# Three additions of products moved into transfers, and two sets of statistics moved to ScalarE

## The chip, the cores and the metric

One Trainium2 chip, and of it one core. The time is the device time of one execution of the whole program in microseconds (us); the smaller is the better. "The median" is that of several executions of one build. The profiled execution is one more, recorded by the hardware profiler.

## What is computed

Two preactivation layers over x of shape (8, 64, 64, 256) in float32. Layer 0 is a deformable convolution with 9 taps, 32 groups of 8 channels, and a grid of offsets and masks made by a depthwise convolution and a projection; layer 1 is a convolution with binarised weights and inputs. Both work on the input after group normalisation and add their result to it.

```python
x = x + dcn(gn(x))        # layer 0
x = x + bin_conv(gn(x))   # layer 1

def dcn(x):               # H = W = 64, G = 32, GC = 8, K = 3
    xdw    = depthwise3x3(x) + dw_b
    om     = xdw @ om_w + om_b                # 27 planes a group: 18 offsets, 9 masks
    value  = x @ vp_w + vp_b
    py, px = base + tap + offset
    sampled = bilinear(value, py, px)         # four neighbours, 0 outside the image
    out    = sum_k sampled_k * mask_k         # over the 9 taps
    return out @ op_w

def gn(v, G=32, eps=1e-5):                    # mean and variance over an image's pixels
    return (g - mean(g)) / sqrt(var(g) + eps) # and the 8 channels of a group
```

## The kernel before

Layer 0 takes 3400 of the 3858 us, in `layer0`. Each of the 8 images is cut into 4 steps (n, j), 32 steps in all. A step has 256 pixel columns (TOK) of each of the 4 quarters of the image, and 9 taps k = 0 to 8. The partitions hold 32 groups for each of the 4 quarters. Offsets stay within one pixel of the tap, so that the 9 taps with their neighbours fall on 5 x 5 shifts: the kernel makes one weight plane for each shift (`wsum`) and then 25 products uv = 0 to 24 of `val` and such a plane, which TensorE adds up. If an offset is larger, another routine, `layer0_any_offset`, would do the work instead; here it doesn't run.

Every engine has its own program, written out in the order in which it runs, and they meet at semaphores. In one step:

- **VectorE**, for each tap k: `mask_rows` (L965) multiplies the weights of a tap in y by its mask, `products` (L979) multiplies them by those in x, straight into `wsum` where a shift is new and into `prod` where one is already there. For taps 1, 2, 3, 6, 7 (`SENT_TAPS`) the part in `prod` is added to `wsum` by a transfer; for 4, 5 and 8 by VectorE (L1007). The products of the next tap wait for it. Between these pieces `multiply` (L1026) makes two or three of the 25 products a tap: `SAMPLES_AT` says which. Products 0 to 12 are made in taps 4 to 8 and 13 to 24 in taps 0 to 3 of the step that follows; product 12 is the last instruction of a step. Each product, 128 x 2048 elements, goes into one of 4 buffers of `pv` in turn and waits until TensorE has read what was there.
- VectorE also takes statistics: in tap 0 four rows over `xres` for the group normalisation of layer 1 (`statistics`, L1036), and in steps 0, 1 and 2 of an image four rows for each half of 128 channels of the next image (`sums_ahead`, L925), loaded ahead into `acc` and `acc_t`; a chain of small instructions (`scales_ahead`) turns these into scales.
- **TensorE**, for each tap: two offset products for the tap after next (`offsets`, L751), the first addition of this tap (`add`, L796: 16 transposing matmuls into PSUM), the third offset product, then one unit of the depthwise convolution of the next step (taps 0 to 3, L722) or of its values (taps 4, 5, 7, 8, L735; one unit each, two each in the last step of an image), the transposition back (tap 4, L764) and the projection (taps 5 and 6, L777), and last the other additions of the tap.
- **ScalarE**, for each tap: the hats, that is the weights in x and y, from the offset products two taps ahead (L585 to L599), then the evictions of TensorE's depthwise, value, transposed and projected units, and the normalisation of the input for the depthwise convolution (`tri`, L540: four instructions of 1024 elements in tap 8, four of 512 in taps 1 and 2). In tap 4 it evicts the 25-fold sum into `acc` (`summed`, L606).
- **GpSimd** issues the transfers that add: `wsum` += `prod` (L472), `xres` += x (L462), and the loads of the image ahead (L455). **SyncE** issues the other loads and the stores of the result, x2.

Layer 1 follows, after all images of layer 0; the change does not touch it.

## Time and profile before

| | us |
|---|---|
| median of 3 executions | 3857.94 |
| lowest, highest of them | 3854.49, 3858.15 |
| the profiled execution, its own time | 3859.76 |
| its span in the trace | 3858.0 |
| TensorE, VectorE, ScalarE, GpSimd busy | 3628.5, 3510.0, 2286.0, 565.0 |
| transfers | 470.35 MB |

In the rows below, PE is TensorE's matmuls, PEld its weight loads, DVE is VectorE, ACT is ScalarE, POOL is GpSimd. L1026 is line 1026 of the kernel. A row of a window gives the stretch in us from the start of the span and its length; then for each engine the busy us and, in brackets, the number of instructions; then the granted TensorE clock as a share of full speed, the mean busy share of the 16 DMA engines, and GB/s. A group of instructions gives line, engine, operation, what is written from what, the shapes and the count; after the first bar the busy us and the mean ns of one; after the second the idle time just before them and who ended it. A row of the timeline gives start and duration in us, the engine, the line and the instruction, and in square brackets the idle time before it with its releaser. Durations overlap the next row by a tenth of a microsecond or so, so that distances are taken from start to start. A GB/s row gives the rate in 40 equal slices of its window.

### The profile page before, as it was taken

What the parts mean: (1) busy time and instruction counts of PE and PEld (TensorE: products, weight loads), DVE (VectorE), ACT (ScalarE), POOL (GpSimd) and SP (SyncE); (2) the same over time, 40 slices, a digit from 0 to 9 for tenths busy, and PEclk for the clock granted to TensorE, in tenths of its full rate; (3) what the DMA queues carried; (4) which work ended last, traced back from release to release, by engine and by line L of the source; (5) the groups of instructions that cost most, each with busy time, mean ns of one, the idle gap of its engine ahead of it and who ended that gap; (6) DMA issues with size and microseconds to landing.
All of it is one profiled execution on the core that took longest, in us unless ns stands there. A gap on an engine that the chain in (4) does not pass through costs nothing. (4 is left out here: it accounts for less than half of the span.)

```text
span 3858.0 us, 90635 instructions
## 1 busy us (share of the span) xinstructions
PE 3628.5 (94%) x37696; PEld 2369.5 (61%) x37696; DVE 3510.0 (91%) x2757; ACT 2286.0 (59%) x4547; POOL 565.0 (15%) x412
## 2 busy tenths in 40 slices
PE   4899999999999999999999999999999999858998
PEld 2566666666666666666666666666666666623333
DVE  4899999999999999999999999989999999948776
ACT  5556665666666665666556666665566666235554
POOL 0011111101111111111111001111111111104444
PEclk9999999999999999999999999999999999979999
DMA  6454565445555555455545555555544554345563
GB/s 177 100 111 102 110 125 132 101 111 116 124 120 109 114 123 115 94 108 127 131 99 119 112 121 114 107 122 131 118 100 97 106 107 94 52 158 199 209 215 147
DMA packets 319939, 470.35 MB, mean 122 GB/s; under 512 B 37244, under 2 KB 242684, under 8 KB 313736
## 3 DMA queue, kind: packets, MB, share of 16 engines
q0 software_dynamic: 94080, 196.11, 28.4%
q1 hardware_dynamic: 224584, 266.07, 23.2%
q8 instruction: 298, 4.88, 0.5%
q10 hardware_dynamic: 832, 2.10, 0.1%
q14 instruction: 145, 1.19, 0.1%
HBM read 262.53 MB, written 67.41 MB: 86 GB/s over the span
## 5 line engine op out<-in xcount | busy, mean ns | idle before, releaser
L1026 DVE TENSOR_TENSOR pv<-val,wsum 128x2048 f32<-128x2048 f32 x800 | 1811.2, 2286 | 21.4 <-ACT xdw L557 14.6
L796 PEld LDWEIGHTS ps_add<-ident,pv 128*128 128x128 f32 x12800 | 1401.2, 142 | 356.0 <-issue 223.7
L796 PE MATMUL ps_add<-ident,pv 128*128 128x128 f32 x12800 | 1527.2, 275 | 70.9 <-DVE pv L1026 62.7
L751 PE MATMUL ps_om<-xdw,omw 128*32 128x256 f32 x13824 | 868.4, 384 | 30.4 <-ACT hat L587 29.4
L585 ACT ACTIVATE hat<-ps_om,omb 128x256 f32<-128x256 f32 x576 | 276.0, 479 | 551.2 <-PE ps_om L751 501.9
L979 DVE TENSOR_TENSOR prod<-hat,mwy 128x1536 f32<-128x1536 f32 (+1 forms) x384 | 526.0, 1397 | 82.9 <-DMA wsum<-prod 61.8
L472 POOL DMA_DIRECT2D wsum<-prod x192 | 226.0, 1254 | 2556.8 <-DVE wsum L979 2556.8
L751 PEld LDWEIGHTS ps_om<-xdw,omw 128*32 128x32 f32 x13824 | 391.2, 109 | 330.2 <-issue 95.5
L589 ACT ACTIVATE msk<-ps_om,omb 128x256 f32<-128x256 f32 x288 | 137.0, 476 | 401.4 <-PE ps_om L751 399.3
L965 DVE TENSOR_TENSOR mwy<-hat,msk 128x768 f32<-128x768 f32 x288 | 274.4, 953 | 94.3 <-ACT hat L599 94.3
L722 PE MATMUL ps_bg<-tri,diag 128*32 128x512 f32 x3024 | 346.5, 592 | 11.9 <-ACT tri L551 11.9
L540 ACT ACTIVATE tri<-tri,gn_tri 96x1024 f32<-96x1024 f32 (+1 forms) x376 | 330.0, 951 | 4.7 <-ACT gn_tri L508 4.5
L735 PE MATMUL ps_bg<-win,vpw 128*32 128x256 f32 x4992 | 294.4, 381 | 0.0
L587 ACT ACTIVATE hat<-ps_om,omb 128x256 f32<-128x256 f32 x576 | 281.4, 489 | 0.0
L586 ACT ACTIVATE hat<-ps_om,nomb 128x256 f32<-128x256 f32 x576 | 276.7, 480 | 0.0
L979 DVE TENSOR_TENSOR wsum<-hat,mwy 128x768 f32<-128x768 f32 (+2 forms) x288 | 257.3, 893 | 2.4 <-DVE pv L1026 1.0
L777 PE MATMUL ps_bg<-acc_t,opw 128*128 128x512 f32 x512 | 238.4, 606 | 1.8 <-ACT acc_t L614 0.7
L735 PEld LDWEIGHTS ps_bg<-win,vpw 128*32 128x32 f32 x4992 | 162.8, 111 | 108.9 <-issue 2.5
L1007 DVE TENSOR_TENSOR wsum<-wsum,prod 128x1536 f32<-128x1536 f32 x192 | 226.0, 1219 | 0.0
L1730 POOL TENSOR_TENSOR c_x<-c_x,c_res 128x1024 f32<-128x1024 f32 x64 | 170.4, 2666 | 341.4 <-ACT c_res L1614 341.4
L722 PEld LDWEIGHTS ps_bg<-tri,diag 128*32 128x32 f32 x3024 | 98.6, 111 | 185.6 <-issue 164.6
L1683 PE MATMUL ps_p<-c_over,c_kw 128*128 128x512 bf16 x768 | 189.5, 397 | 19.9 <-ACT c_res L1608 19.9
(134 smaller groups left out, 2622.7 us busy)
## 6 DMA issues: line engine op xcount, KB each, us to landing
wsum<-prod POOLq DMA_DIRECT2D x160, 768.0 KB, 7.1
tri<-in_x_dram SPq DMA_DIRECT2D x725, 128.0 KB, 2.9
win<-in_x_dram SPq DMA_DIRECT2D x144, 256.0 KB, 3.6
x<-xres SPq DMA_DIRECT2D x128, 256.0 KB, 5.1
xres<-in_x_dram POOLq DMA_DIRECT2D x124, 256.0 KB, 8.4
out_dram<-c_x SPq DMA_DIRECT2D x31, 1024.0 KB, 4.5
c_x<-x SPq DMA_DIRECT2D x30, 1024.0 KB, 5.3
c_box<-box_d SPq DMA_DIRECT2D x16, 1024.0 KB, 7.4
```

The costliest lines, as they stand in the source:

```text
L540: last = nc.scalar.activation(v, v, ACT.Identity, bias=gn_tri[0:KROWS, j % 2, 2 * c + 1, h:h + 1], scale=gn_tri[0:KROWS, j % 2, 2 * c, h:h ...
L585: nc.scalar.activation(hat[:, par, a, 1, :], d, ACT.Abs, bias=b).then_inc(abs_done, 1)
L586: nc.scalar.activation(hat[:, par, a, 0, :], d, ACT.Relu, bias=nb, scale=-1.0)
L587: nc.scalar.activation(hat[:, par, a, 2, :], d, ACT.Relu, bias=b).then_inc(om_free, 1)
L722: mm = nc.tensor.matmul(out[:, :, :, o0:o1], diag[:, h, c, kx, :], src, start=kx == 1, stop=kx == 2)
L735: mm = nc.tensor.matmul(ps_bg[G * q:G * q + G, par, ci * TOK:(ci + 1) * TOK], vpw[:, h, 2 * cp + ci, :], win_of(n, j, i // V_UNITS)[:, h, ...
L751: mm = nc.tensor.matmul(ps_om[G * q:G * q + G, (par + i) % 2, 0:TOK], omw[:, h, comp, :], xdw[:, j % 2, h, q, :], start=h == 0, stop=h == ...
L777: mm = nc.tensor.matmul(ps_bg[:, par, :], opw[:, h, P * oh:P * oh + P], acc_t[:, h, 512 * tb:512 * tb + 512], start=h == 0, stop=h == CH - 1)
L796: mm = nc.tensor.matmul(ps_add[:, tb, c, :], pv[:, (j + uv) % PBUF, c, P * tb:P * tb + P], consts["ident"][:, :], start=uv == 0 and c % 4 ...
L965: nc.vector.tensor_tensor(mwy[:, :, :], hat[:, par, 1, :, :], msk[:, par, :].unsqueeze(1).to_broadcast([P, 3, TOK]), ALU.mult)\
L979: return nc.vector.tensor_tensor(dst, hat[:, par, 0, c:d, :].unsqueeze(1).to_broadcast(shape), mwy[:, a:b, :].unsqueeze(2).to_broadcast(sh ...
L1026: nc.vector.tensor_tensor(pv[:, (j + uv) % PBUF, :, :].rearrange("p c (r w) -> p c r w", w=W), val[:, :, SR * j + u:SR * j + u + SR, v:v + ...
```

## The change

Four things change, all in layer 0.

Products 0 and 1, 2 and 3, and 10 and 11 are added in pairs by a transfer within `pv` (`add_pair`), issued by GpSimd, before TensorE sees the sum; TensorE adds 22 times instead of 25. `pv` has five buffers, and product uv goes into buffer uv modulo 5. The product that takes the buffer of the first of a pair (5, 7, 15) waits for the transfer; every other one waits for TensorE's addition of what lies there (16 for the addition of the sum of 10 and 11).

Both sets of statistics are taken by ScalarE, each as one pass for the sum and one for the sum of squares, in place of VectorE's rows: those of the image ahead at the end of taps 7 and 0 (`sums_ahead`), those of `xres` at the end of taps 1 and 2 (`statistics`). The image ahead has only one buffer, `acc_t`, so its second half is loaded after the first has been summed, and both halves after the fourth projection. The sums of products are evicted into `xres` (`acc` is a view of it), so that eviction waits for the stores of x2 from there.

The order of the additions is written out in `ADDS_AT`, apart from that of the products.

```diff
-PBUF = 4
+PBUF = 5
+PAIRED = {1: 0, 3: 2, 11: 10}
+PAIRS = list(PAIRED)
+ADDS_AT = [(13, 14, 11, 15), (16, 17, 18), (19, 20, 21), (22, 23, 24), (), (1,), (4, 3, 5, 6), (7, 8, 9), (12,)]
...
+                def add_pair(n, j, uv):
+
+                    s = STEPS * n + j
+                    pool.wait_ge(pv_full, SHIFTS * s + uv + 1)
+                    at_least(pool, pair_added, 16 * (len(PAIRS) * s + PAIRS.index(uv)))
+                    nc.gpsimd.dma_start(pv[:, (SHIFTS * j + uv) % PBUF, :, :], pv[:, (SHIFTS * j + PAIRED[uv]) % PBUF, :, :],
+                                        accum_op=ALU.add).then_inc(pair_added, 16)
...
                         for k in SENT_TAPS:
+                            if k == 6:
+                                add_pair(n, j, 1)
+                                add_pair(n, j, 3)
+                            add_products(n, j, k)
                             if k == 6 and j < CH and n < NI - 1:
-                                load_ahead(n, j, 0, "back3")
-                            add_products(n, j, k)
+                                load_ahead(n, j, 0, "project3")
+                        if (n, j) != (0, 0):
+                            add_residual(*previous(n, j), unit(n, j, "project3", NI) + 1)
                         if j < CH and n < NI - 1:
                             load_ahead(n, j, 1, "project3")
-                        if (n, j) != (0, 0):
-                            add_residual(*previous(n, j), unit(n, j, "project3", NI) + 1)
+                        add_pair(n, j, 11)
...
                 def summed(s):
-                    act.wait_ge(add_done, SHIFTS * (s + 1))
+                    act.wait_ge(add_done, ADDS * (s + 1))
+                    at_least(act, x2_stored, 16 * Q * s)
...
+                    for oh in halves:
+                        for i, kind in ((0, ACT.Identity), (1, ACT.Square)):
+                            nc.scalar.activation(spare[:, :, :], xres[:, oh, :, :], kind, bias=pivot2[:, oh:oh + 1],
+                                                 accum_out=x2_sums[:, oh, i, j:j + 1]).then_inc(stats2, 1)
+                            act.wait_ge(stats2, 2 * CH * s + 2 * oh + i + 1)
...
+                    nc.scalar.activation(ahead, ahead, ACT.Identity, bias=pivot[:, j:j + 1],
+                                         accum_out=x_sums[:, half, j, 0:1]).then_inc(centred, 1)
+                    act.wait_ge(centred, i + 2 + half)
+                    nc.scalar.activation(ahead, ahead, ACT.Square, accum_out=x_sums[:, half, j, 1:2]).then_inc(sums_made, 1)
...
+                        if k == AHEAD_AT and j < CH and has_next(n):
+                            sums_ahead(n, j, 0)
+                        if k == 0 and j in (1, 2) and has_next(n):
+                            sums_ahead(n, j - 1, 1)
+                        if k in (1, 2) and not is_step(n, j, 0, 0) and not is_step(n, j, 0, 1):
+                            statistics(*previous(*previous(n, j)), (k - 1,))
...
-                    if not isinstance(s, int) or s > 0 or uv >= PBUF:
-                        dve.wait_ge(add_done, SHIFTS * s + uv - PBUF + 1)
+                    used, in_step = (uv - PBUF, s) if uv >= PBUF else (uv - PBUF + SHIFTS, s - 1)
+                    if used in PAIRED.values():
+                        dve.wait_ge(pair_added, 16 * (len(PAIRS) * in_step + list(PAIRED.values()).index(used) + 1))
+                    elif not isinstance(s, int) or in_step >= 0:
+                        dve.wait_ge(add_done, ADDS * in_step + ADDED.index(used) + 1)
```

TensorE's program at the end of a step, before: taps 7 and 8 and the start of tap 0 of the next step. L751 are offset products, L796 additions (16 matmuls each), L735 a unit of values, L722 the depthwise unit.

```order
L796 MATMUL ps_add<-ident,pv 128x128 x32
L751 MATMUL ps_om<-xdw,omw 32x256 x16
L796 MATMUL ps_add<-ident,pv 128x128 x16
L751 MATMUL ps_om<-xdw,omw 32x256 x8
L735 MATMUL ps_bg<-win,vpw 32x256 x16
L796 MATMUL ps_add<-ident,pv 128x128 x32
L751 MATMUL ps_om<-xdw,omw 32x256 x16
L796 MATMUL ps_add<-ident,pv 128x128 x16
L751 MATMUL ps_om<-xdw,omw 32x256 x8
L722 MATMUL ps_bg<-tri,diag 32x512 x4
L722 MATMUL ps_bg<-tri,diag 32x8x63 x8
L796 MATMUL ps_add<-ident,pv 128x128 x32
```

The same place in the changed kernel, where L861 are the additions, L813 the offset products, L797 the values and L784 the depthwise unit:

```order
L861 MATMUL ps_add<-ident,pv 128x128 x32
L813 MATMUL ps_om<-xdw,omw 32x256 x16
L861 MATMUL ps_add<-ident,pv 128x128 x16
L813 MATMUL ps_om<-xdw,omw 32x256 x8
L797 MATMUL ps_bg<-win,vpw 32x256 x16
L813 MATMUL ps_om<-xdw,omw 32x256 x16
L861 MATMUL ps_add<-ident,pv 128x128 x16
L813 MATMUL ps_om<-xdw,omw 32x256 x8
L784 MATMUL ps_bg<-tri,diag 32x512 x4
L784 MATMUL ps_bg<-tri,diag 32x8x63 x8
L861 MATMUL ps_add<-ident,pv 128x128 x48
```

Tap 8 had three additions, 10 ahead of the third offset product and 11 and 12 behind the values; now it has one, 12, ahead of the third offset product, and tap 0 has four, 13 early and 14, 11, 15 at its end.

GpSimd's program for one step with a load ahead, before: taps 1 and 2 in the first row, then tap 3, a load, taps 6 and 7, a load and the residual.

```order
L472 DMA wsum<-prod 128x3x512 x2
L472 DMA wsum<-prod 128x2x768
L455 DMA acc<-in_x_dram 128x2048
L472 DMA wsum<-prod 128x2x768 x2
L472 DMA wsum<-prod 128x512
L455 DMA acc_t<-in_x_dram 128x2048
L462 DMA xres<-in_x_dram 128x2x256 x4
```

The same in the changed kernel, with the semaphores that each row waits for:

```order
L487 DMA wsum<-prod 128x3x512 [waits wsum_added,prod_done] x2
L487 DMA wsum<-prod 128x2x768 [waits wsum_added,prod_done]
L495 DMA pv<-pv 128x2048 [waits pair_added,pv_full] x2
L487 DMA wsum<-prod 128x2x768 [waits wsum_added,prod_done]
L470 DMA acc_t<-in_x_dram 128x2048 [waits bg_full]
L487 DMA wsum<-prod 128x2x768 [waits wsum_added,prod_done]
L487 DMA wsum<-prod 128x512
L477 DMA xres<-in_x_dram 128x2x256 [waits bg_free]
L477 DMA xres<-in_x_dram 128x2x256 x3
L470 DMA acc_t<-in_x_dram 128x2048 [waits sums_made,bg_full]
L495 DMA pv<-pv 128x2048 [waits pair_added,pv_full]
```

Two pairs now stand ahead of tap 6's transfer, the first load ahead has moved behind it, and the third pair stands at the end of the step, behind the residual and the second load.

## Rows read from the trace of the kernel before

**Rows 1.** The page, busy time of the engines (share of the span, instructions)
```profile
PE 3628.5 (94%) x37696; PEld 2369.5 (61%) x37696; DVE 3510.0 (91%) x2757; ACT 2286.0 (59%) x4547; POOL 565.0 (15%) x412
```
**Rows 2.** Windows: 27 steps; product 16 to step's end; a stretch of layer 1
```profile
255.00:3050.98 2795.98, 2719.48 (x30269) 1859.71 (x30262) 2665.73 (x1999) 1739.81 (x3616) 336.99 (x294) 1.00 0.53 114
...
1213.59:1300.28 86.69, 85.70 (x978) 57.83 (x980) 81.12 (x57) 54.17 (x112) 11.97 (x10) 1.00 0.57 121
...
3500.00:3512.00 12.00, 8.33 (x32) 3.23 (x31) 11.90 (x13) 2.38 (x4) 3.31 (x2) 0.86 0.75 260
```
**Rows 3.** VectorE's groups of instructions in those 27 steps, 255 to 3051 us
```profile
L1026 DVE TENSOR_TENSOR pv<-val,wsum 128x2048 f32<-128x2048 f32 x675 | 1528.8, 2285 | 6.5 <-PE ps_add L796 6.4
L979 DVE TENSOR_TENSOR prod<-hat,mwy 128x1536 f32<-128x1536 f32 (+1 forms) x324 | 443.8, 1397 | 74.1 <-DMA wsum<-prod 60.5 <-issue 9.0 <-DVE var L950 1.2
...
L1036 DVE BATCH_NORM_STATS2 bs<-xres 128x6 f32<-128x512 f32 x108 | 66.6, 679 | 0.8
L925 DVE BATCH_NORM_STATS2 bs<-acc_t 128x6 f32<-128x512 f32 x52 | 32.1, 680 | 0.0
...
L1052 DVE TENSOR_REDUCE scratch<-over_sum 128x1 f32<-128x9 f32 x28 | 4.3, 155 | 0.0
```
**Rows 4.** Timeline, VectorE: start of a step, its product 16, start of the next
```profile
1198.73 2.56 DVE L979 TENSOR_TENSOR wsum<-hat,mwy 128x2304 f32<-128x2304 f32 x1
...
1208.68 2.46 DVE L1036 BATCH_NORM_STATS2 bs<-xres 128x6 f32<-128x512 f32 x4
...
1213.59 2.28 DVE L1026 TENSOR_TENSOR pv<-val,wsum 128x2048 f32<-128x2048 f32 x1
...
1300.46 2.56 DVE L979 TENSOR_TENSOR wsum<-hat,mwy 128x2304 f32<-128x2304 f32 x1 [0.18 <-DVE pv L1026]
```
**Rows 5.** Timeline, TensorE: tap 8 of one step, tap 0 of the next
```profile
1404.55 1.91 PE L735 MATMUL ps_bg<-win,vpw 128*32 128x256 f32 x32
1406.39 3.71 PE L796 MATMUL ps_add<-ident,pv 128*128 128x128 f32 x32
...
1411.89 1.97 PE L796 MATMUL ps_add<-ident,pv 128*128 128x128 f32 x16
1413.79 1.07 PE L751 MATMUL ps_om<-xdw,omw 128*32 128x256 f32 x16
1414.68 2.73 PE L722 MATMUL ps_bg<-tri,diag 128*32 128x512 f32 x24
1417.34 3.71 PE L796 MATMUL ps_add<-ident,pv 128*128 128x128 f32 x32
```
**Rows 6.** Timeline: ScalarE's `tri` blocks and hats at that place; TensorE waiting for hats
```profile
1407.76 4.64 ACT L540 ACTIVATE tri<-tri,gn_tri 96x1024 f32<-96x1024 f32 x4 [0.20 <-ACT gn_tri L508]
1412.31 0.45 ACT L585 ACTIVATE hat<-ps_om,omb 128x256 f32<-128x256 f32 x1
...
1206.59 0.45 ACT L585 ACTIVATE hat<-ps_om,omb 128x256 f32<-128x256 f32 x1
...
1207.81 1.07 PE L751 MATMUL ps_om<-xdw,omw 128*32 128x256 f32 x16 [1.42 <-ACT hat L587]
```
**Rows 7.** Timeline, VectorE: products of taps 4, 8, 6 and 7, waits for transfers
```profile
932.50 2.36 DVE L979 TENSOR_TENSOR prod<-hat,mwy 128x1536 f32<-128x1536 f32 x2 [0.79 <-DMA wsum<-prod]
...
770.73 2.36 DVE L979 TENSOR_TENSOR prod<-hat,mwy 128x1536 f32<-128x1536 f32 x2 [1.46 <-DMA wsum<-prod]
...
1263.94 1.75 DVE L979 TENSOR_TENSOR prod<-hat,mwy 128x1536 f32<-128x1536 f32 x1
...
1274.46 2.36 DVE L979 TENSOR_TENSOR prod<-hat,mwy 128x1536 f32<-128x1536 f32 x2 [0.42 <-DMA wsum<-prod]
```
**Rows 8.** A transfer's median time to landing; tap 7's transfers, issue, and window 1277.4:1286
```profile
wsum<-prod POOLq DMA_DIRECT2D x160, 768.0 KB, 7.1
...
1277.45 2.12 POOL L472 DMA_DIRECT2D wsum<-prod  x2 [9.40 <-DVE wsum L979]
...
GB/s 0 0 0 0 0 0 0 38 171 186 143 214 186 186 214 157 214 186 214 171 186 171 200 214 214 200 181 143 181 219 210 162 181 133 19 10 10 76 0 0
```

159 lines of the change are left out of this document (88 added, 71 removed).

## The prediction, made before the changed kernel was run

> **What bounds the kernel now.** I read the page's busy shares first: TensorE 94%, VectorE 91%, ScalarE 59% [rows 1]. Two nearly full engines mean that neither may be shortened alone, so next come the windows. The 27 steps between the first and last VectorE row that ends a step (the group of 28 in [rows 3]) take 2796.0 us, so 103.55 us a step; in them TensorE is busy 2719.5 (100.7 a step) and VectorE 2665.7 (98.7 a step) [rows 2]. What VectorE waits for there is small and mostly the transfers that add into `wsum`: 60.5 us in all, 2.2 a step [rows 3]. So both engines are close to the bound in turn, and a cheaper step needs both to get shorter and the order of their handshakes to stay harmless. I therefore follow one step on three engines. T0 is the moment at which VectorE has finished product 12, the last of its step, and starts tap 0 of the next.
>
> **What is removed.** VectorE loses its statistics: the 108 rows on `xres` are 66.6 us (2.5 a step), and those on the image ahead are 52 of the kind shown and 48 more like it on `acc`, 61.7 us together (2.3 a step) [rows 3]. That is 4.8 of 98.7. TensorE loses 3 of 25 additions, at 1.85 to 1.90 us each [rows 5], so 5.6 of 100.7. Were nothing added, TensorE would need 95.1 and VectorE 93.9 a step, about 8 us below today.
>
> **What is added on ScalarE.** Four passes over 1024 elements a step for the second statistics and eight over 2048 an image for the first. From its 1024-element rows (four in 4.64 us, 1.14 apart [rows 6]) and a read of the accumulator each, I take 1.35 and 2.5 us: 5.4 + 5.0 = 10.4 us a step on an engine that is 59% busy. They stand behind the depthwise or value evictions of taps 0, 1, 2 and 7, where ScalarE has been waiting for TensorE. A delayed `hat` delays TensorE, which, as worked out below, will have some 8 us of slack a step; I cost them at nothing, and up to 1 us a step if that cover is gone. The new wait of the eviction of the sums on the stores of x2 (they share `xres`) holds what is queued behind it on ScalarE, the hats of tap 6 and the values; by the same slack it costs nothing, and 1 us without it.
>
> **The new wait on the path: product 16 for addition 11.** With five buffers product 16 goes where the sum of products 10 and 11 lies, so VectorE waits until TensorE has added it. In the new order TensorE adds 12 early in tap 8, ahead of the third offset product of the next tap 1 and of the values, and then 13, 14, 11, 15 in tap 0. All of that now stands behind T0, since product 12 is what VectorE makes last. From T0: 0.3 to see the product; addition 12, 1.90; third offsets, 0.89; one value unit, 1.84 [rows 5]: the values end at T0 + 4.9. In the kernel before, two additions followed here, and beside them ScalarE evicted the values and scaled four `tri` blocks before its next hats: from the end of the values (the row at 1406.39) to those hats (1412.31) are 5.9 us [rows 5, 6]. Now no additions cover this. The hats start at T0 + 10.8, and TensorE's third offsets of tap 0 follow 1.22 later (1206.59 to 1207.81, a row that shows this very wait) [rows 6], at T0 + 12.1. Then 0.89 for them, 2.66 for the depthwise and 1.85 each for 14 and 11 [rows 5]: addition 11 ends at T0 + 19.3, and product 16 can start at **T0 + 19.4**. VectorE on its own reaches product 16 at 1213.59 - 1198.73 = 14.86 after T0, less the 2.39 of the four removed statistics rows between, 12.5 [rows 4]. The wait is 6.9 us, every step. It is certain in kind, as the semaphore's count and the order say so, and its size is made of rows.
>
> **From product 16 to the next T0** VectorE's own work is 81.1 us (busy in 1213.59 to 1300.28) [rows 2]. To it come waits. For tap 4 it waits for the transfer of the tap before, 0.79 where it runs unhindered; tap 3 has the same work and transfer before it, so I take 0.79 again; and tap 8 waits 1.46 [rows 7]. In the kernel before these show only in part of the steps, because there TensorE often held VectorE anyway. I take all three, 3.0.
>
> **The transfers of the pairs.** Each adds 1 MiB within `pv`. No row shows one. The nearest is tap 7's two transfers, also 1 MiB with an addition and mostly runs of 3 KB: issued at 1277.45, bytes move from 1279.1 to 1284.7 at some 188 GB/s (slices 9 to 34 of the 40 in 1277.4 to 1286) [rows 8]. With 1.7 ahead and some 1.2 behind (768 KB alone land in 7.1 [rows 8]: 1.7 + 4.2 + 1.2) a pair lands 8.5 after its issue. Pair 1 is issued at the end of tap 4 and has a tap of 10.1 us: hidden. Pair 11 has 13 us until product 15: hidden. Pair 3 is issued after product 3, and 2.5 us later tap 6's 768 KB go into the same queue behind it; tap 7's products wait for those. They land 0.3 + 1.7 + 5.6 + 4.2 + 1.2 = 13.0 after product 3, while VectorE needs 10.1 (1263.94 to 1274.46 less the 0.42 waited) [rows 7]: a wait of 2.9. Bounds: 0.4, as now, if the two run abreast; 6 if 1 MiB takes half as long again and pair 1 is late for pair 3. I take 2.9, made of the nearest row. GpSimd's queue is otherwise harmless: the load of the first half now waits for the fourth projection, ahead of tap 7's transfers, but that ends some 3 us before tap 7's products do.
>
> **Small terms.** The longer chains of one-column instructions and the two value units in every fourth step: 0.8 and 0.5 (1.84 / 4) a step.
>
> **The sum.** 19.4 + 81.1 + 3.0 + 2.9 + 1.3 = 107.7 us a step against 103.55, 4.15 more. TensorE alone would need 95.1 and the 3.4 that it waits for the hats (they let its offsets start 7.2 after the values, two offsets and addition 13 take 3.8), 98.5. So it has the slack of 9 us used above, and stands idle for some 7 of them before addition 12. Some 30 step boundaries: +125 us; the end, where statistics no longer run between the last residual additions, +3. The profiled execution (3859.8) becomes 3987, and the median, 1.8 below it, **3985 us**. Layer 1 is not touched.
>
> **Rivals.**
> - **Pair 3 hidden.** The two transfers overlap, or contiguous 8 KB rows add faster. The wait of 2.9 falls to 0.4: 30 x 2.5 = 75 less, 3910. For it: the rows show no two such transfers queued right behind each other at full length. Against it: within tap 7's transfers the bytes run at an even rate to the end, as they do when the transfer itself is what limits [rows 8]. The Trainium skill, DMA: Bandwidth & Descriptors, section "Anatomy of one DMA — SWDGE (gpsimd) path", gives a fit of 2.0 us + bytes / 436 GB/s for a transfer of this path, 4.4 us for 1 MiB; by that the 5.9 us of waits for transfers would drop out of the sum, and the time would be about 3810. The trace disagrees for transfers that add: 768 KB take 7.1, where the fit says 3.8; I give that outcome 0.01 of the faster case below. Pair 3 hidden has a chance of 0.16, nearly all of it at 3880 to 3950.
> - **Faster: VectorE's own work decides.** The point is the time from T0 to the end of addition 11. Under 15.2 us instead of 19.4 the step is shorter than today, and under 12.5 the wait is gone: 12.5 + 81.1 + 0.8 (a wait for tap 1's transfer, now in the open) + 3.0 + 2.9 + 1.3 = 101.6, 30 x 1.95 = 58 less than before and 3 more at the end, **3803**. It needs ScalarE to have its `tri` blocks done earlier than the order says, or VectorE's last product not to be what addition 12 waits for. For it: both busy engines lose 5 us of work. Against it: the chain above has no part without a row. Chance 0.16; within 0.2% another 0.04.
> - **Worse.** After TensorE's idle time of 7 us the granted clock may fall. In 3500 to 3512, where it was busy 8.3 of 12 us, the mean was 0.86 [rows 2], which is 3.4 us at the lower level (1.2 GHz) of the two; on this path that costs 1.7 us a step. With it pair 1 late and pair 3 with it, +3: 30 x 4.7 = 141 more than the forecast, 4126. Chance 0.17.
>
> **How the numbers follow.** The forecast, 3950 to 4050 by itself, has 0.47; pair 3 hidden 0.16; worse 0.17; no change 0.04; faster 0.16. Leaving out the faster case and the far end of the worse one is 2 in 10: the range is 3850 to 4120. About 0.2% (8 us) is what a measurement of this kernel can tell from no change. Faster 0.16, same 0.04, slower 0.80.
>
> **What would show it.** Right: VectorE's product rows waiting for additions some 6 to 7 us once a step (6.4 us in all 27 steps now, on that line); TensorE idle some 7 us before one addition a step, on VectorE's product; its third offsets of tap 0 waiting 3 us for ScalarE's hats; VectorE's `prod` rows waiting for transfers some 6 us a step; a step of 107 to 108 us; VectorE busy about 87% in layer 0. Wrong: product 16 starting without a wait, or a step under 103 us, would fell the main term; a wait of tap 7 under 1 us would fell that of the pairs. What would make it wrong in size is a transfer of a pair that lands in 6 or in 12 us instead of 8.5, or a ScalarE that holds up TensorE for longer than its slack.

## The result, and the profile after

The changed kernel takes 4096.06 us (median of 4 executions, 4085.68 to 4100.32) against 3858.05 for the kernel before (4 executions, 3854.49 to 3864.67): ratio 1.0611, with a 95% interval of 1.0593 to 1.0629. It is slower by 238 us. The forecast was slower, 3985 us, with a range of 3850 to 4120; the sign and the main mechanism held, and the size was 111 us short. The profiled execution took 4085.68 us, with a span of 4083.9; the steps below are measured on it.

The page of the changed kernel: busy times (the line of before is in [rows 1]), and the granted clock in 40 slices.

```profile
PE 3536.7 (87%) x36160; PEld 2252.7 (55%) x36160; DVE 3371.2 (83%) x2555; ACT 2552.1 (62%) x4937; POOL 650.6 (16%) x508
...
PEclk9899999999999999999999999999999999979999
```

Both full engines lost work, as intended, and the time rose. The 27 steps that [rows 2] gave for the kernel before (2796.0 us, TensorE busy 2719.5, VectorE 2665.7) read now, in the same columns (us, PE, PEld, DVE, ACT, POOL, clock, DMA share, GB/s):

```profile
266.90:3251.35 2984.45, 2645.07 (x28985) 1759.05 (x28984) 2544.05 (x1823) 1972.24 (x3955) 409.63 (x376) 0.96 0.64 136
```

That is 110.5 us a step against 103.55, so 7.0 more; the 27 steps make 188 of the 226 us by which the span grew. VectorE is busy 94.2 us a step (forecast 93.9), TensorE 98.0 (forecast 95.1), and its mean clock fell from 1.00 to 0.96.

What VectorE waited for in these steps (line, releaser: us in total, times, longest):

```profile
DVE pv L1090 <- PE ps_add L861: 247.4, 39, 10.8
DVE prod L1040 <- DMA wsum<-prod: 115.9, 67, 3.9
DVE mwy L1026 <- ACT hat L626: 39.6, 22, 2.7
DVE wsum L1040 <- issue: 19.0, 5, 3.8
```

In the kernel before the first of these lines was 6.4 us [rows 3]. In tap 1, where product 16 stands, there are 27 of the 39 waits, one a step, 228.4 us together: 8.5 us a step, forecast 6.9. The last of these lines, five waits of 3.8 us with no releaser in the trace, stands behind the last step of an image, between the end of product 12 and the first row of tap 0. What it is stays open; what it does to the sums stands below the table. And what TensorE waited for:

```profile
PE ps_om L813 <- ACT hat L614: 165.0, 101, 5.2
PE ps_add L861 <- DVE pv L1090: 157.6, 28, 8.2
```

One step boundary shows the chain. VectorE's rows of it, with T0 = 1159.3, where product 12 ends and tap 0 begins (start and duration in us; in brackets the idle time before the row and its releaser):

```profile
1157.02 2.28 DVE L1090 TENSOR_TENSOR pv<-val,wsum 128x2048 f32<-128x2048 f32 x1
1159.34 2.56 DVE L1040 TENSOR_TENSOR wsum<-hat,mwy 128x2304 f32<-128x2304 f32 x1
1161.81 2.28 DVE L1090 TENSOR_TENSOR pv<-val,wsum 128x2048 f32<-128x2048 f32 x1
1166.84 0.96 DVE L1026 TENSOR_TENSOR mwy<-hat,msk 128x768 f32<-128x768 f32 x1 [2.74 <-ACT hat L626]
1167.71 4.49 DVE L1090 TENSOR_TENSOR pv<-val,wsum 128x2048 f32<-128x2048 f32 x2
...
1183.63 2.29 DVE L1090 TENSOR_TENSOR pv<-val,wsum 128x2048 f32<-128x2048 f32 x1 [8.89 <-PE ps_add L861]
```

TensorE's rows of the same stretch: addition 12, the third offsets, the values, two offsets for the tap after next, addition 13, the third offsets of tap 0, the depthwise unit, and the start of additions 14 and 11.

```profile
1149.71 1.93 PE L813 MATMUL ps_om<-xdw,omw 128*32 128x256 f32 x32
1159.36 3.68 PE L861 MATMUL ps_add<-ident,pv 128*128 128x128 f32 x16 [7.71 <-DVE pv L1090]
1162.96 1.94 PE L813 MATMUL ps_om<-xdw,omw 128*32 128x256 f32 x16
1164.67 2.25 PE L797 MATMUL ps_bg<-win,vpw 128*32 128x256 f32 x32
1166.75 1.90 PE L813 MATMUL ps_om<-xdw,omw 128*32 128x256 f32 x32
1168.58 1.97 PE L861 MATMUL ps_add<-ident,pv 128*128 128x128 f32 x16
1174.63 1.07 PE L813 MATMUL ps_om<-xdw,omw 128*32 128x256 f32 x16 [4.08 <-ACT hat L614]
1175.52 4.43 PE L784 MATMUL ps_bg<-tri,diag 128*32 128x512 f32 x24
```

The order of events is the one forecast, each in its place: TensorE idle 7.7 us before addition 12, the third offsets of tap 0 waiting for ScalarE's hats, product 16 waiting for an addition. The sizes differ in three rows. Addition 12 takes 3.6 us to the next row where [rows 5] had 1.85 to 1.90, the third offsets behind it 1.7 where it had 0.89, and the depthwise unit 4.36 where it had 2.66. From T0 to product 16 are 24.3 us here, forecast 19.4. The granted clock in windows of 4 us says why (same columns as above):

```profile
1149.50:1153.50 4.00, 2.15 (x35) 0.99 (x33) 4.00 (x3) 4.00 (x8) 0.58 (x1) 1.00 0.63 109
1153.50:1157.50 4.00, 0.00 (x0) 0.00 (x0) 4.00 (x5) 0.07 (x1) 0.86 (x1) 0.70 0.98 301
1157.50:1161.50 4.00, 2.14 (x10) 2.14 (x11) 3.96 (x2) 0.00 (x0) 0.00 (x0) 0.50 0.94 195
1161.50:1165.50 4.00, 4.00 (x36) 2.37 (x38) 2.60 (x2) 0.53 (x2) 0.00 (x0) 0.52 0.00 0
1165.50:1169.50 4.00, 4.00 (x68) 2.44 (x61) 2.66 (x2) 3.60 (x9) 0.00 (x0) 1.00 0.29 81
...
1177.50:1181.50 4.00, 4.00 (x31) 2.06 (x24) 0.00 (x0) 1.59 (x3) 0.00 (x0) 0.81 1.03 178
```

TensorE stood idle from 1151.6; its clock fell from 2.4 to 1.2 GHz within that time, and addition 12, the third offsets and the start of the values ran at the lower level. It was back at 1.00 from 1165.5, and fell a second time about a microsecond after the 4.1 us in which TensorE had waited for the hats: the third offsets of tap 0 still took their usual 1.07 us, the depthwise unit ran slow. These windows show it:

```profile
1174.00:1175.00 1.00, 0.37 (x8) 0.28 (x12) 0.73 (x1) 1.00 (x4) 0.00 (x0) 1.00 0.00 0
1176.00:1177.00 1.00, 1.00 (x8) 0.22 (x4) 0.00 (x0) 0.97 (x4) 0.30 (x1) 0.50 0.14 25
```

The transfers of the pairs, and those that add 768 KB, on the page (KB each, median us from issue to landing):

```profile
wsum<-prod POOLq DMA_DIRECT2D x160, 768.0 KB, 7.2
pv<-pv POOLq DMA_DIRECT2D x96, 1024.0 KB, 7.2
```

A pair lands in 7.2 us (6.9 to 9.2), not 8.5.

### The profile page after: what moved, and what is told of

The parts are those of the page before. It is cut to its first block and busy times, and to the rows that moved or that the text cites. A ratio compares the mean times of both kernels' runs of the same rounds, so it can differ in the third digit from the quotient of the medians.

```text
span 4083.9 us, 88179 instructions
## 1 busy us (share of the span) xinstructions
PE 3536.7 (87%) x36160; PEld 2252.7 (55%) x36160; DVE 3371.2 (83%) x2555; ACT 2552.1 (62%) x4937; POOL 650.6 (16%) x508
## 5 line engine op out<-in xcount | busy, mean ns | idle before, releaser
L861 PE MATMUL ps_add<-ident,pv 128*128 128x128 f32 x11264 | 1368.9, 280 | 205.8 <-DVE pv L1090 205.5
L861 PEld LDWEIGHTS ps_add<-ident,pv 128*128 128x128 f32 x11264 | 1268.6, 144 | 450.4 <-DVE pv L1090 236.4
L813 PE MATMUL ps_om<-xdw,omw 128*32 128x256 f32 x13824 | 896.6, 394 | 211.7 <-ACT hat L614 210.5
L813 PEld LDWEIGHTS ps_om<-xdw,omw 128*32 128x32 f32 x13824 | 399.9, 111 | 546.9 <-ACT hat L614 264.6
L784 PE MATMUL ps_bg<-tri,diag 128*32 128x512 f32 x3024 | 376.3, 634 | 11.9 <-ACT tri L578 11.9
L797 PE MATMUL ps_bg<-win,vpw 128*32 128x256 f32 x4992 | 296.4, 383 | 0.0
L495 POOL DMA_DIRECT2D pv<-pv x96 | 84.3, 878 | 1043.0 <-DVE pv L1090 1043.0
L797 PEld LDWEIGHTS ps_bg<-win,vpw 128*32 128x32 f32 x4992 | 163.4, 112 | 113.2 <-issue 8.0
L784 PEld LDWEIGHTS ps_bg<-tri,diag 128*32 128x32 f32 x3024 | 106.0, 120 | 215.2 <-issue 198.2
```

The lines of the kernel that those rows point to most:

```text
L784: mm = nc.tensor.matmul(out[:, :, :, o0:o1], diag[:, h, c, kx, :], src, start=kx == 1, stop=kx == 2)
L797: mm = nc.tensor.matmul(ps_bg[G * q:G * q + G, par, ci * TOK:(ci + 1) * TOK], vpw[:, h, 2 * cp + ci, :], win_of(n, j, i // V_UNITS)[:, h, ...
L813: mm = nc.tensor.matmul(ps_om[G * q:G * q + G, (par + i) % 2, 0:TOK], omw[:, h, comp, :], xdw[:, j % 2, h, q, :], start=h == 0, stop=h == ...
L861: mm = nc.tensor.matmul(ps_add[:, tb, c, :], pv[:, (SHIFTS * j + uv) % PBUF, c, P * tb:P * tb + P], consts["ident"][:, :], start=uv == ADD ...
```

## The experiments

Twelve kernels. "Step" is the mean of the same 27 steps; the next two columns split it, from the rows of VectorE, into the time from T0, here the start of the first row of tap 0, to the start of product 16 and from there to the next T0. The forecast for the changed kernel was 107.7 = 19.4 + 88.3.

| kernel | median us | ratio to before, 95% | step | T0 to 16 | 16 to T0 |
|---|---|---|---|---|---|
| before | 3858 to 3860 | 1 | 103.6 | 16.5 | 87.0 |
| changed | 4096.1 | 1.0611 (1.0593 to 1.0629) | 110.5 | 22.6 | 88.0 |
| e1_late | 3870.0 | 1.0035 (1.0024 to 1.0047) | 103.2 | 15.2 | 88.1 |
| e2_busy | 4093.1 | 1.0611 (1.0592 to 1.0629) | 110.8 | 22.6 | 88.2 |
| e5_fill | 4051.5 | 1.0499 (1.0481 to 1.0516) | 109.0 | 20.8 | 88.3 |
| e6_stats | 4104.2 | 1.0640 (1.0623 to 1.0658) | 110.8 | 22.5 | 88.4 |
| e7_swap | 4111.5 | 1.0658 (1.0641 to 1.0676) | 111.3 | 22.8 | 88.5 |
| e12_no3 | 4115.5 | 1.0666 (1.0648 to 1.0684) | 111.7 | 22.4 | 89.3 |
| e11_after_loads | 4106.0 | 1.0644 (1.0626 to 1.0662) | 110.9 | 22.7 | 88.3 |
| e3_two | 3800.7 | 0.9854 (0.9838 to 0.9871) | 101.2 | 12.5 | 88.7 |
| e4_none | 3872.2 | 1.0038 (1.0024 to 1.0051) | 103.9 | 12.7 | 91.2 |
| e8_loads | 3820.1 | 0.9899 (0.9882 to 0.9915) | 102.2 | 12.7 | 89.4 |
| e9_two_loads | 3795.0 | 0.9827 (0.9811 to 0.9844) | 100.9 | 12.5 | 88.4 |
| e10_one_loads | 3804.8 | 0.9855 (0.9839 to 0.9872) | 101.7 | 12.7 | 89.0 |

The 3.8 us with no releaser lie between the end of product 12 and that first row, in five of the 27 steps of the changed kernel, of e1_late, e2_busy, e5_fill, e6_stats, e7_swap, e12_no3 and e11_after_loads; the other kernels have not more than 0.5 us there. The chain starts when product 12 ends, since addition 12 waits for that and not for tap 0. Counted from there, the changed kernel takes 23.3 us to product 16 and 87.2 for the rest, e5_fill 21.5 and 87.5. Where the chain is held against the forecast below, these numbers are used. In the changed kernel VectorE still waited 4.5 to 7.7 us for addition 11 in these steps, so that they cost it next to nothing there.

### Is it the place of addition 12, and the pair 10, 11?

**e1_late** moves addition 12 behind the third offsets and the values.

```diff
-                        before = [uv for uv in ADDS_AT[k][:1] if uv not in PAIRED]
+                        before = [uv for uv in ADDS_AT[k][:1] if uv not in PAIRED and k != TAPS - 1]
```

> Only the place of addition 12 changes: in tap 8 TensorE takes it after the third offset product and the values, no longer ahead of them. Theory A (the wait of product 16 is a chain that hangs on addition 12 standing ahead of the values): the values and ScalarE's scaling of tri lie before T0 again, so from T0 the chain is 0.3 + addition 12 1.9 + two offsets 1.9 + addition 13 1.9 + third offsets 0.9 + depthwise 2.7 + additions 14 and 11 3.7 = 13.3 to 14.2 us, against VectorE's own 12.5. The wait of product 16 falls from 9.2 us to 1 to 2, the step from 110.5 to about 102, the time to 3810 to 3830 us (ratio 0.99 to kernel before). Rival (the waits for transfers and the pairs hold the step, and a shorter chain only hands its time to them): the step stays above 106 us, the time above 3930 (ratio over 1.02).

This one line took 7.3 us off the step, where the change had added 7.0: T0 to product 16 fell from 22.6 to 15.2, and the other part of the step stayed at 88.1. So the chain is what costs the time, and nothing took its place. The size was missed by 40 us. One part is the chain, 15.2 us against my 14.2 at most: behind the last step of an image the two value units now run past the end of product 12 and hold addition 12, so that from that end to product 16 are 17.8 to 19.5 us there and 14.0 to 15.6 elsewhere. TensorE also still waits for hats (78.8 us in the 27 steps) and for products (88.8), and its clock falls in most steps (mean 0.98). I did not split the rest. At 103.2 us a step the kernel is no better than before.

**e3_two** undoes the third pair.

```diff
-PAIRED = {1: 0, 3: 2, 11: 10}
-ADDS_AT = [(13, 14, 11, 15), (16, 17, 18), (19, 20, 21), (22, 23, 24), (), (1,), (4, 3, 5, 6), (7, 8, 9), (12,)]
+PAIRED = {1: 0, 3: 2}
+ADDS_AT = [(13, 14, 15), (16, 17, 18), (19, 20, 21), (22, 23, 24), (), (1,), (4, 3, 5, 6), (7, 8, 9), (10, 11, 12)]
...
-                        add_pair(n, j, 11)
```

> The third pair (10 and 11) is undone: TensorE adds 10, 11 and 12 in tap 8 in the places they had in the kernel before, 23 additions in all; pairs 1 and 3, the five buffers and the statistics on ScalarE stay. Theory A (the pair of 10 and 11, added by TensorE only after T0, is what costs the time): product 16 then takes the buffer of product 11, added before T0, and doesn't wait. A step is VectorE's own 12.5 + 81.1 and the waits for transfers and pairs, 3.0 + 2.0 to 2.9 + 1.3, so 100 to 101 us; the time 3765 to 3800 us, ratio 0.976 to 0.985. Rival (ScalarE's statistics and the transfers of pairs 1 and 3 cost most of what was lost): 106 us a step or more, over 3930 us.

Product 16 no longer waits: T0 to 16 is 12.5 us in each of the 27 steps, which is VectorE's own work as forecast. Two pairs and ScalarE's statistics make the kernel 1.5% faster than before, one pair more makes it 6% slower. The window of the 27 steps, and VectorE's main wait in them:

```profile
256.20:2988.20 2732.00, 2616.84 (x29407) 1760.03 (x29408) 2541.79 (x1823) 1969.21 (x3952) 386.13 (x349) 1.00 0.65 138
```

```profile
DVE prod L1039 <- DMA wsum<-prod: 141.9, 79, 6.8
```

TensorE has 96.9 us of work a step, one addition more than the changed kernel and 1.0 us less busy time, because its clock stays at 1.00. VectorE's 94.1, these 5.3 us a step of waits for transfers, and 1.8 us of other idle time make the step of 101.2.

### Is it the clock?

**e2_busy** does the second offset product of tap 8 seven times, with the same result each time, to fill TensorE's idle time before addition 12.

```diff
-                    for h in range(CH):
-                        for q in range(Q):
+                    for _ in range(7 if (k, i) == (1, 1) else 1):
+                        for h in range(CH):
+                            for q in range(Q):
```

> The changed kernel, and in tap 8 TensorE does the second offset product (8 matmuls of 256 columns, 0.9 us) seven times instead of once, with the same result each time, just before addition 12. That fills 5.5 us of the 7.7 us in which it waits there for product 12; 5.5 us a step of matmuls are added. Theory A (the granted clock falls because TensorE stood idle, and the lower clock lengthens the chain behind T0): addition 12 takes 1.9 us again instead of 3.6, the depthwise unit of tap 0 2.7 instead of 4.4, the granted clock in the 8 us after T0 is near 1.0, and the step falls by 3 to 4.5 us, to 106 to 107.5, so the time to 3960 to 4000 us (ratio 1.027 to 1.037) although TensorE has more work. Rival B (the clock isn't what lengthens the chain, or falls for another reason): no change within 10 us of the changed kernel's 4096, ratio 1.06. Rival C (the added matmuls cost their time): 4096 + up to 32 x 5.5 = up to 4270.

Nothing moved: 4093. That would have spoken against the clock, but the trace shows two flaws of the experiment. At the next boundary (T0 = 1271.3) addition 12 ran at full speed, the clock was 1.00 up to 1283, and it fell in the second idle stretch, which I had not filled. TensorE's rows there, and windows of 4 us:

```profile
1271.35 1.96 PE L862 MATMUL ps_add<-ident,pv 128*128 128x128 f32 x16 [1.45 <-DVE pv L1091]
1284.85 1.93 PE L814 MATMUL ps_om<-xdw,omw 128*32 128x256 f32 x16 [5.19 <-ACT hat L614]
1286.56 4.69 PE L784 MATMUL ps_bg<-tri,diag 128*32 128x512 f32 x24
```

```profile
1281.00:1285.00 4.00, 0.15 (x4) 0.15 (x8) 3.15 (x3) 3.91 (x7) 0.56 (x1) 0.83 0.06 22
1285.00:1289.00 4.00, 4.00 (x28) 1.23 (x28) 0.00 (x0) 2.67 (x7) 0.72 (x1) 0.50 0.75 129
```

So part of the loss only changed its place, and in 7 of the 27 steps addition 12 still ran slow. Of the 124 depthwise units with all their 24 matmuls in the trace, which take 2.73 us, 28 took over 3 us here, 28 in the changed kernel, none in the kernel before. The second flaw: behind the last step of an image TensorE has two value units and hardly an idle time to fill, so that the repeated matmuls run past the end of product 12 and hold addition 12. From the end of product 12 to product 16 are 21.5, 22.5 and 22.8 us behind an image's first, second and third step (22.2, 23.2 and 25.2 in the changed kernel), and 26.4 behind its last (22.6). The gain in three steps was paid back in the fourth.

**e5_fill** fills both.

```diff
-                    for h in range(CH):
-                        for q in range(Q):
+                    for _ in range({(1, 1): 8, (2, 1): 4}.get((k, i), 1)):
+                        for h in range(CH):
+                            for q in range(Q):
```

> In the run with the second offset product done seven times the step stayed at 110.8 us: TensorE didn't lose its clock before addition 12 in every other step, but stood idle 4 to 5 us before the third offsets of tap 0 (waiting for ScalarE's hats) and took 4.7 us for the depthwise unit behind it at the lower level of the clock. Here both idle stretches are filled with repeated offset products of the same result: the one of tap 8 is done 8 times, the second one of tap 0 4 times (2.7 us more, ahead of addition 13). Theory A (the lower clock lengthens the chain from T0 to addition 11 by 1.7 at addition 12, 0.8 at the third offsets, 1.7 at the depthwise unit): all of the step is at a granted clock near 1.0, addition 12 takes 1.9 and the depthwise unit 2.7, the wait of product 16 falls from 9.2 to 5 to 7 us, the step from 110.5 to 106 to 108; 3960 to 4030 us, ratio 1.027 to 1.045. Rival (the wait is set by the order of the work alone, the clock only by the wait): 4085 to 4110, ratio 1.06.

More work on TensorE (103.8 us busy a step instead of 98.0) and 45 us less time: the intervals of the two ratios are apart. The same boundary as shown above for the changed kernel, with T0 = 1150.7 (TensorE's rows, then VectorE's product 16, then the window of the 27 steps):

```profile
1150.71 1.97 PE L862 MATMUL ps_add<-ident,pv 128*128 128x128 f32 x16 [2.15 <-DVE pv L1091]
1152.61 1.07 PE L814 MATMUL ps_om<-xdw,omw 128*32 128x256 f32 x16
1153.50 1.91 PE L797 MATMUL ps_bg<-win,vpw 128*32 128x256 f32 x32
...
1163.10 1.07 PE L814 MATMUL ps_om<-xdw,omw 128*32 128x256 f32 x16 [1.48 <-ACT hat L614]
1163.99 2.73 PE L784 MATMUL ps_bg<-tri,diag 128*32 128x512 f32 x24
...
1170.40 2.29 DVE L1091 TENSOR_TENSOR pv<-val,wsum 128x2048 f32<-128x2048 f32 x1 [6.88 <-PE ps_add L862]
```

```profile
269.90:3213.60 2943.70, 2801.37 (x33324) 1861.04 (x33322) 2545.05 (x1823) 1974.19 (x3956) 409.65 (x376) 1.00 0.65 138
```

With the clock at 1.00 (2 of the 124 depthwise units took over 3 us), product 16 waits 6.88 us and starts 19.7 after T0. The forecast for this chain, made of rows of the kernel before, was 6.9 and 19.4. So the chain was right at full clock.

The mean of 20.8 in the table understates what the clock costs, since behind the last step of an image the repeated matmuls hold addition 12 here too. TensorE's rows at such a boundary, where product 12 ended at 930.8, then a window of the changed kernel at one where the clock did not fall, from the end of product 12 to the start of product 16:

```profile
927.69 7.98 PE L814 MATMUL ps_om<-xdw,omw 128*32 128x256 f32 x144
935.60 1.97 PE L862 MATMUL ps_add<-ident,pv 128*128 128x128 f32 x16
```

```profile
2269.95:2290.79 20.84, 17.41 (x218) 11.95 (x219) 12.58 (x9) 13.79 (x28) 1.28 (x1) 1.00 0.36 93
```

Taken by the step of the image that ends, from the end of product 12 to the start of product 16 (mean of the changed kernel; the boundaries with the clock at 1.00 throughout, of e5_fill for the first three, of the changed kernel itself for the last; and all of e5_fill):

| behind an image's step | changed | at full clock | e5_fill |
|---|---|---|---|
| first | 22.2 | 19.1 | 19.1 |
| second | 23.2 | 19.7 | 19.7 to 21.4 |
| third | 25.2 | 20.9 | 20.8 to 22.6 |
| last | 22.6 | 20.8 (2 of 7) | 23.6 to 25.9 |

The full-clock column averages 20.2 over the 27 steps, the changed kernel 23.3. The difference, 3.1 us a step, is an estimate of what the lower clock costs. e5_fill gives back 1.8, since it gains 3 to 4 us in three steps and loses 2.4 in the fourth.

### Do ScalarE's statistics cost anything?

**e6_stats** lets ScalarE take both statistics over an eighth of the elements, with the means scaled to that.

```diff
-                            nc.scalar.activation(spare[:, :, :], xres[:, oh, :, :], kind, bias=pivot2[:, oh:oh + 1],
+                            nc.scalar.activation(spare[:, 0, 0:128], xres[:, oh, 0, 0:128], kind, bias=pivot2[:, oh:oh + 1],
...
-                    nc.scalar.activation(ahead, ahead, ACT.Identity, bias=pivot[:, j:j + 1],
+                    part = ahead[:, 0:256]
+                    nc.scalar.activation(part, part, ACT.Identity, bias=pivot[:, j:j + 1],
```

> Part of the computation is left out: ScalarE takes both statistics over an eighth of the elements (128 of 1024 and 256 of 2048 a partition), and the means are scaled to that. ScalarE's added work falls from 10.4 us a step to about 3. Theory A (in the changed kernel this work stands beside other waits and costs nothing, as predicted): within 15 us of the changed kernel's 4096, ratio 1.057 to 1.062. Rival (it delays hats and evictions that others wait for): up to 7 us a step less, so down to 3880, ratio 1.005.

ScalarE was busy 5.8 us a step less (1815.2 us in the 27 steps against 1972.2), and the time was not shorter but 4104: this much of that work costs nothing in the changed kernel. The statistics take 9.5 us a step there by their rows, so 3.7 were not taken away and not tested.

### The pairs in GpSimd's queue

**e7_swap** issues the pair 2, 3 behind tap 6's transfer, and TensorE adds its sum last in tap 6.

```diff
-ADDS_AT = [(13, 14, 11, 15), (16, 17, 18), (19, 20, 21), (22, 23, 24), (), (1,), (4, 3, 5, 6), (7, 8, 9), (12,)]
+ADDS_AT = [(13, 14, 11, 15), (16, 17, 18), (19, 20, 21), (22, 23, 24), (), (1,), (4, 5, 6, 3), (7, 8, 9), (12,)]
...
                             if k == 6:
                                 add_pair(n, j, 1)
-                                add_pair(n, j, 3)
                             add_products(n, j, k)
+                            if k == 6:
+                                add_pair(n, j, 3)
```

> The transfer of the pair 2, 3 is issued behind tap 6's transfer instead of ahead of it, and TensorE adds its sum last in tap 6 instead of second. Theory A (the prediction's term of the pairs: tap 7's products wait for tap 6's transfer only because 1 MiB stands before it in the same queue): tap 7's wait of 1.8 to 2.0 us goes, the step falls from 110.5 to 108.5 to 109, the time to 4035 to 4060, ratio 1.046 to 1.052. Rival B (the two transfers share the memory's rate whichever comes first, or TensorE's chain makes the step anyway): within 15 us of 4096. Rival C (the pair now lands too late for product 7, or TensorE waits for it with the hats' offsets behind): slower than 4110.

The waits moved, and grew. Tap 7's wait for tap 6's transfer (51.5 us in the 27 steps of the changed kernel) is nearly gone (2.7), and product 7 waits for the pair instead; product 8 waits 28.0 us for TensorE's additions, where it waited 5.8, and tap 8's wait falls from 47.5 to 28.7:

```profile
DVE pv L1091 <- DMA pv<-pv: 64.1, 27, 3.5
DVE prod L1041 <- DMA wsum<-prod: 51.4, 37, 4.5
```

**e12_no3** drops the pair 2, 3; TensorE adds 2 and 3 in tap 5.

```diff
-PAIRED = {1: 0, 3: 2, 11: 10}
-ADDS_AT = [(13, 14, 11, 15), (16, 17, 18), (19, 20, 21), (22, 23, 24), (), (1,), (4, 3, 5, 6), (7, 8, 9), (12,)]
+PAIRED = {1: 0, 11: 10}
+ADDS_AT = [(13, 14, 11, 15), (16, 17, 18), (19, 20, 21), (22, 23, 24), (), (2, 3, 1), (4, 5, 6), (7, 8, 9), (12,)]
...
-                                add_pair(n, j, 3)
```

> The changed kernel without the pair 2, 3: TensorE adds 2 and 3 itself in tap 5 (23 additions), pairs 0, 1 and 10, 11 stay. Theory A (the pair ahead of tap 6's transfer costs tap 7's wait, on average 1.8 to 2 us): tap 7's wait goes, and this time nothing else waits for the pair, as it did when the two transfers changed places; the step falls to 108.5 to 109, 4035 to 4060 us, ratio 1.046 to 1.053. Prediction's term of 2.9: 108.0, 4020 (1.042). Rival (what VectorE saves there it waits for elsewhere): within 15 us of 4096.

Slower by 20 us than the changed kernel, where I expected some 50 less. Tap 7's wait is nearly gone (2.8), but tap 8 waits 111.3 us in the 27 steps where it waited 47.5, 91 of them in the steps with a load ahead, and product 6 waits 35.0 for TensorE where it waited 13.2. TensorE's extra additions in tap 5 push the projections back, GpSimd waits for the fourth one before the load of the image ahead, and tap 7's transfers are queued behind it:

```profile
1482.18 0.58 POOL L470 DMA_DIRECT2D acc_t<-in_x_dram  x1 [12.87 <-PE ps_bg L838]
1482.75 2.15 POOL L487 DMA_DIRECT2D wsum<-prod  x2
...
1494.94 2.36 DVE L1039 TENSOR_TENSOR prod<-hat,mwy 128x1536 f32<-128x1536 f32 x2 [9.05 <-DMA wsum<-prod]
```

**e4_none** shows the same queue without any pair.

```diff
-PAIRED = {1: 0, 3: 2, 11: 10}
-ADDS_AT = [(13, 14, 11, 15), (16, 17, 18), (19, 20, 21), (22, 23, 24), (), (1,), (4, 3, 5, 6), (7, 8, 9), (12,)]
+PAIRED = {}
+ADDS_AT = SAMPLES_AT
...
-                                add_pair(n, j, 1)
-                                add_pair(n, j, 3)
...
-                        add_pair(n, j, 11)
```

> No pair is added by transfer: 25 additions in the places of the kernel before. What is left of the change is the statistics on ScalarE, five buffers instead of four, and the sums in the residual's buffer. Theory A (ScalarE's added work of 10.4 us a step costs nothing): VectorE has 94 us of work a step, TensorE 100.7 and some waits for hats, so TensorE holds the step at 101.5 to 102.5 us; 3795 to 3830 us, ratio 0.984 to 0.993. Rival (ScalarE's added work delays hats and evictions by its own length, as TensorE has no slack here): up to 103.5 + 5, ratio 1.0 to 1.04.

3872 us, 14 more than before and 42 more than the top of what I expected, though VectorE has 4.5 us a step less to do. The steps take 104, 97, 104 and 111 us in turn. In the longest GpSimd waits 17.6 us for the projection (1391.77) and VectorE then 8.36 for tap 7's transfers (1403.49):

```profile
1391.77 0.58 POOL L470 DMA_DIRECT2D acc_t<-in_x_dram  x1 [17.55 <-PE ps_bg L835]
1392.34 2.14 POOL L487 DMA_DIRECT2D wsum<-prod  x2
...
1403.49 2.36 DVE L1036 TENSOR_TENSOR prod<-hat,mwy 128x1536 f32<-128x1536 f32 x2 [8.36 <-DMA wsum<-prod]
```

**e8_loads** is e4_none with these loads issued by SyncE.

```diff
-                    nc.gpsimd.dma_start(ahead, src[:, HW // 2 * half:HW // 2 * (half + 1)]).then_inc(x_ahead[half], 16)
...
+                    if j < CH and has_next(n):
+                        if not first:
+                            sp.wait_ge(bg_full, unit(n, j, "project3", NI) + 1)
+                        src = x_v[n + 1][:, j].rearrange("p r w -> p (r w)")
+                        for half in range(2):
+                            if half == 1:
+                                sp.wait_ge(sums_made, CH * CH * n + CH * j + 1)
+                            sp.dma_start(ahead, src[:, HW // 2 * half:HW // 2 * (half + 1)]).then_inc(x_ahead[half], 16)
```

> As the kernel without pairs (25 additions in the old places, statistics on ScalarE, five buffers: 3872 us), but the loads of the image ahead are issued by SyncE instead of GpSimd. In that kernel GpSimd waited up to 17 us for the fourth projection ahead of that load in the steps 0 and 1 of an image, with tap 7's transfers queued behind; VectorE then waited 7 to 9 us for them, and the steps took 104, 97, 104 and 111 us in turn. Theory A (that queue costs what the relieved VectorE should have given): the waits of 7 to 9 us are gone, the steps are even, and the time falls to 3810 to 3840, ratio 0.988 to 0.995. Rival (TensorE's own 100.7 us and its 3 us of waits make the step, the queue's delay is caught up in the next one): 3860 to 3875, ratio 1.000 to 1.004.

3820: the queue had cost 52 us. VectorE's waits for transfers in the 27 steps, in e4_none and in e8_loads:

```profile
DVE prod L1036 <- DMA wsum<-prod: 128.1, 44, 9.3
```

```profile
DVE prod L1029 <- DMA wsum<-prod: 20.5, 26, 2.7
```

**e11_after_loads** makes the same move in the changed kernel, with its three pairs.

> The changed kernel with all three pairs, and only the loads of the image ahead moved from GpSimd's queue to SyncE's. Theory A (as the prediction had it: in the changed kernel TensorE is early, the fourth projection ends before tap 7's products, so GpSimd's wait for it holds nothing): within 15 us of 4096, ratio 1.057 to 1.065. Rival (as in the kernel without pairs, where it cost 52 us): 4040 to 4060, ratio 1.047 to 1.052.

4106: no gain there. In the changed kernel GpSimd does wait for the projection (110.0 us, 12 times), but each of these waits ends 0.8 to 2.8 us before tap 7's products do, about as forecast (some 3): the change has its harmless cover only while TensorE is early. In e12_no3 none of the same waits left such a margin.

### Better versions

**e9_two_loads** is e3_two with SyncE's loads, **e10_one_loads** the same with the pair 0, 1 alone (`PAIRED = {1: 0}`, additions 1, 2, 3 in tap 5).

> Pairs 1 and 3 only, and the loads of the image ahead issued by SyncE. With two pairs and GpSimd issuing the loads the time was 3801 and every fourth step took 104.5 us against 100, with a wait of 6 us for tap 7's transfers. Theory A (those waits are GpSimd's wait for the fourth projection): the steps are even at 100 us, 3765 to 3780 us, ratio 0.975 to 0.980. Rival (the wait comes from the pairs' bytes or the long step behind an image): 3795 to 3805, ratio 0.985.

> Only the pair 0, 1 is added by transfer (24 additions), loads by SyncE. Theory A (TensorE holds the step without pairs: 100.7 of work and 1.4 of waits made 102.2 us, and VectorE's 94 us and its waits for transfers hold it with two): one pair takes 1.87 off TensorE and costs VectorE nothing, since no pair stands ahead of tap 6's transfer: 100.3 us a step, ratio 0.975 to 0.980, as good as two pairs. Rival (each pair's 1 MiB slows the transfers that add to wsum, whatever its place): 102 us a step or more, ratio 0.988 or above.

e9_two_loads is the fastest of all, 3795.0 us, 1.7% below the kernel before. The two missed the top of what I expected by 15 and by 22 us. In e9_two_loads the waits of taps 7 and 8 stayed for the most part (54.5 and 54.9 us in the 27 steps against 51.8 and 67.7 in e3_two): with two pairs they come mainly from the transfers themselves, not from GpSimd's wait for the projection. In e10_one_loads VectorE hardly waits for transfers (13.0 us), but waits for hats (121.0) and, with product 6, for TensorE (40.5), and TensorE waits for hats in turn (68.7). Whether ScalarE's statistics lengthen these waits for hats was not tested.

## Why the prediction was right, point by point

**The bound and the removed work** were right. TensorE without clock losses needs 95.1 us a step by the forecast; with one addition more it measures 96.9 in e3_two. VectorE's 93.9 measures 94.2.

**The main term, product 16 for addition 11,** was right as a mechanism and at full clock nearly also in size: 6.88 us and T0 + 19.7 at the boundary shown of e5_fill, against 6.9 and T0 + 19.4, and 20.2 as the mean of the full-clock column above. Undoing it by either of two edits (e1_late, e3_two) took the loss away.

**What the sum got wrong is the clock in this chain.** It took the durations of [rows 5], all at 2.4 GHz, although the prediction itself said that TensorE would stand idle for some 7 us. It named the consequence only in the rival "worse", with a chance of 0.17, and priced it at 1.7 us a step. Both the chance and the price were too low. What the prediction put as "may fall" came nearly every time: 26 single additions in the trace follow a wait of over 3 us for a product; all took 2.4 us or more where full clock takes 1.97, and 24 over 3. And the clock falls twice in the chain, which the rival did not have: a second time behind TensorE's wait for the hats, 3 to 5 us, where the prediction had that wait (3.4 us) but no slower row behind it. In 25 of the 27 steps the depthwise unit of tap 0 was slow. Together that is 3.1 us a step, by the estimate above. The other half of that rival, pair 1 late by 3 us, did not happen, since a pair lands in 7.2 us.

**The rest of the chain's excess,** 20.2 against 19.4, depends on the step of the image, as the table above shows: 19.1 us behind its first step, 20.9 behind its third, 20.8 behind its last, where two value units stand in the chain. The forecast was made of one boundary. TensorE's wait for the hats of tap 0 is 3.4 us behind the first step and 5.2 behind the third; what makes that difference was not separated.

**From product 16 to T0** the forecast was 81.1 + 3.0 + 2.9 + 1.3 = 88.3, and 87.2 were measured up to the end of product 12. Inside, the terms shifted: tap 7's wait behind the pair is 1.9 us instead of 2.9 (a pair takes 7.2, not 8.5), tap 8's 1.8 instead of 1.5, tap 3's 0.6 instead of 0.8, tap 4's nothing instead of 0.8, so 4.3 us instead of 5.9. TensorE's hold on products 6 and 8 (0.7 us a step, all of it in the last step of an image) was not in the forecast.

**The rival "pair 3 hidden"** was wrong as a price for an edit: e7_swap and e12_no3 both remove tap 7's wait, and both are slower. The wait is where several releases come close together, and the next one takes its place. By the fit in the Trainium skill, DMA: Bandwidth & Descriptors, section "Anatomy of one DMA — SWDGE (gpsimd) path", 1 MiB would take 4.4 us; the trace has 7.2.

**The rival "VectorE's own work decides"** was priced at 101.6 us a step and 3803 us, from a chain shorter than 12.5. e3_two meets that condition and measures 101.2 and 3800.7. What was missed in it is that the chain is a matter of one pair.

**ScalarE's 10.4 us at nothing** was right as far as tested: 9.5 us were measured, and taking away 5.8 of them gained nothing (e6_stats). **GpSimd's queue harmless** was right for this kernel (e11_after_loads), but only under TensorE's early end of the projections; without the pairs it costs 52 us.

**The sum.** 110.5 - 107.7 is 2.8 us a step: 3.9 more from the end of product 12 to product 16 (some 3.1 the clock, 0.8 the differences between steps) and 1.1 less in the rest. Over some 31 boundaries 2.8 is 88 of the 99 us by which the profiled execution exceeds its forecast of 3987; I did not split the others. The tail behind the last step is 3.0 us longer, forecast 3. That the miss is 2.8 us a step and not 3.9 is luck: the clock that was left out and a rest that was 1.1 us too long partly cancel.

## What to carry to other kernels

Removing work from two full engines gains nothing if the order puts a buffer's release behind the last instruction of a step: find, for each reused buffer, what stands between its last write and its release on every engine, and sum that chain against the writer's own work. If that sum makes TensorE idle for several microseconds, price the rows behind every such idle time of the chain at the lower clock, not only behind the longest one. If you fill idle time as a test, look at the steps that have none to fill: there the added work is on the path. And of several like edits made together, try each alone: with two of these pairs the kernel was 1.5% faster than before, with the third 6.1% slower.

## What the runs showed of the hardware

- Filling TensorE's idle time with repeated matmuls made the kernel 45 us faster, with 5.8 us more matmul time a step: the same 16 transposing matmuls take 1.9 us after an idle time of 2.15 us (clock 1.00) and 3.6 after 7.7 us (clock 0.50).
- Filling one of two idle stretches gained nothing (e2_busy): the clock still fell in the other, at a wait of 5.2 us, and the unit behind it took 4.7 instead of 2.7 us; in the steps without idle time before addition 12 the added matmuls cost 3.8 us.
- The clock need not fall within the wait: at 1174 to 1175 it was still 1.00 after 4.1 us of idle time, and 0.50 at 1176 to 1177, with TensorE busy again.
- A transfer that adds 1 MiB between two buffers of SBUF lands as fast (7.2 us) as one that adds 768 KB in shorter pieces (7.2 us).
